# A fused decoder layer (32 batches, one core): the first and last steps in new orders

## What is computed

```python
x = _layernorm(x + _L0_attn_ref(x, L0_attn_W))                       # 1
x = _layernorm(x + _L0_xattn_ref(x, ctx_1024, ctx_1024, mask, Wq, ...)) # 2
x = _layernorm(x + _L0_ffn_ref(x, L0_ffn_Wr, L0_ffn_Wi, L0_ffn_Wo))  # 3

def _L0_attn_ref(x, W):                 # self attention without projections
    probs = softmax(x @ x.T / 16)
    vacuum_mask = probs < 0.01
    casimir = broadcast(sum of the masked probs) @ W.T
    sparse_probs = where(vacuum_mask, 0, probs), divided by its sum + 1e-9
    return sparse_probs @ x + casimir * 0.01

# 2: q, k, v projections with bias, 16 heads of 16, mask, softmax, output projection
# 3: 8 experts, the best 2 of a softmax over xf @ Wr; x @ Wi[e] @ Wo[e], weighed by their gates
```

## Time and profile before

| | |
|---|---|
| median of 3 runs (lowest, highest) | 748.14 us (746.77, 750.72) |
| the profiled execution: device time, span from first to last instruction | 752.42 us, 750.6 us |
| PE busy | 724.8 us (97%) |
| DVE, ACT, POOL busy | 662.9 (88%), 588.6 (78%), 213.5 (28%) us |
| mean granted TensorE clock | 0.992 of full |
| moved by DMA | 110.84 MB, mean 148 GB/s |

### The profile page before, as it was taken

One profiled execution on the slowest core, in us unless ns is written; L12 is line 12 of the kernel. 1 busy time (PEld: TensorE's weight loads), 2 busy tenths in 40 slices (PEclk: granted clock), 3 DMA queues, 4 the chain that ended last, 5 costly groups with the idle time before them and its releaser, 6 DMA issues.

```text
span 750.6 us, 21145 instructions
## 1 busy us (share of the span) xinstructions
PE 724.8 (97%) x7250; PEld 653.6 (87%) x7250; DVE 662.9 (88%) x2608; ACT 588.6 (78%) x1435; POOL 213.5 (28%) x384
## 2 busy tenths in 40 slices
PE   5889999999999999999999999999999999999996
PEld 4678899999999989999999989999999989889875
DVE  5587889999999889999999989999999989998976
ACT  2378989888888898888888898888988898778730
POOL 7131322133333231333331233333313333341001
PEclk9999999999999999999999999999999999999989
DMA  8865664556655565555555566556545665554100
GB/s 242 245 171 150 190 167 123 152 146 161 163 134 160 142 167 150 146 154 147 156 149 139 152 170 164 142 153 154 142 139 147 163 167 164 133 164 126 29 16 28
DMA packets 75660, 110.84 MB, mean 148 GB/s; under 512 B 14225, under 2 KB 59169, under 8 KB 75553
## 3 DMA queue, kind: packets, MB, share of 16 engines
q1 hardware_dynamic: 75552, 109.49, 54.2%
HBM read 50.23 MB, written 18.35 MB: 91 GB/s over the span
## 4 chain that ended last, share of the span: by engine, by line
PE 88%; SPq 4%; DMA 3%; DVE 3%; ACT 1%; issue 1%; POOL 0%; POOLq 0%; DVEq 0%; ACTq 0%
PE psum L1623 20%; PE psum L1397 12%; PE psum L1431 11%; PE psum L1415 10%; PE psum L1502 4%; PE psum L1490 4%; PE psum L1477 4%; PE psum L1572 3%; PE psum L1535 3%; PE psum L1513 3%; PE psum L1524 3%; SPq L393 2%; PE psum L1553 2%; PE psum L1452 2%; PE psum L1441 2%; DMA k_stack<-k_hi 1%
## 5 line engine op out<-in xcount | busy, mean ns | idle before, releaser
L934 DVE CUSTOM_DVE_ANT_0 scores_left<-psum,mask_add 112x375 f32<-112x375 f32 x512 | 270.5, 542 | 24.6 <-PE psum L1397 17.9
L613 ACT ACTIVATE probsT<-psum 125x448 f32<-125x448 f32 x384 | 201.7, 537 | 17.8 <-PE psum L1415 14.1
L598 ACT ACTIVATE psum<-mask_u 125x448 f32<-125x448 uint8 x372 | 198.2, 541 | 3.7
L1397 PE MATMUL psum<-k_stack,q_stack 96*112 96x376 f32 x512 | 183.1, 365 | 2.6 <-DMA k_stack<-k_hi 1.2
L1415 PE MATMUL psum<-q_stack,k_stack 97*125 97x224 f32 x768 | 148.2, 280 | 2.3 <-ACT psum L598 1.1
L1415 PEld LDWEIGHTS psum<-q_stack,k_stack 97*125 97x125 f32 x768 | 134.7, 188 | 13.1 <-ACT psum L598 2.5
L1166 DVE SCALAR_TENSOR_TENSOR late<-psum,gate,late 128x256 f32<-128x256 f32 x224 | 107.8, 481 | 21.0 <-PE psum L1623 12.3
L562 POOL TENSOR_TENSOR ctx_lo<-ctx_sb,ctx_hi 128x188 fp32r<-128x188 f32 x128 | 71.5, 590 | 126.4 <-ACT ctx_hi L721 126.3
L1397 PEld LDWEIGHTS psum<-k_stack,q_stack 96*112 96x112 f32 x512 | 89.1, 177 | 13.0 <-issue 6.3
L1623 PE MATMUL psum<-we_hi,x_hi 128*128 128x512 f32 x224 | 92.0, 411 | 0.5 <-DVE gate_nmax L1111 0.5
L1623 PE MATMUL psum<-we_hi,x_lo 128*128 128x512 f32 x224 | 89.0, 397 | 0.0
(11 more groups left out here) (169 smaller groups left out, 1622.3 us busy)
## 6 DMA issues: line engine op xcount, KB each, us to landing
k_stack<-k_hi SPq DMA_DIRECT2D x256, 94.0 KB, 2.6
q_stack<-q_scratch SPq DMA_DIRECT2D x96, 224.0 KB, 3.8
ctx_sb<-in_context_T SPq DMA_DIRECT2D x32, 376.0 KB, 3.7
k_stack<-k_lo SPq DMA_DIRECT2D x128, 94.0 KB, 2.5
q_scratch<-q_hi SPq DMA_DIRECT2D x32, 224.0 KB, 2.1
q_scratch<-q_lo SPq DMA_DIRECT2D x32, 224.0 KB, 2.0
xT<-in_x_T SPq DMA_DIRECT2D x32, 112.0 KB, 2.4
x_sb<-in_x SPq DMA_DIRECT2D x32, 112.0 KB, 2.9
```

The source lines that it names most:

```text
L598: nc.scalar.activation(psum[0:KP, ST_BANKS[i % 2], 0:4 * TOK].rearrange("p (h q) -> p h q", h=4), mask_u8[b % MASKS][:, KEYS + t * TOK:KEY ...
L613: nc.scalar.activation(probsT[:, place, i % KT, :], psum[0:KP, ST_BANKS[i % 2], 0:4 * TOK], ACT.Exp, scale=-1.0).then_inc(probs_ready, 1)
L934: nc.vector.tensor_tensor_reduce(scores_left[:, n % 2, :], psum[0:TOK, S_BANKS[n % 2], 0:KEYS], mask_add[b % 2][:, :], 1.0, 3.0e38, ALU.ad ...
L1397: nc.tensor.matmul(psum[0:TOK, S_BANKS[n % 2], 0:KEYS_EVEN], q_stack[s][0:96, pair, odd, c, :], k_stack[s][0:96, pair, c, :], start=True, ...
```

## The change

No arithmetic of the result changes. In the head:

- POOL fills only two of the `k_stack` rows; ACT fills the third as its first instruction, by a copy of a constant (`last_fill_of_ones`, 1 x 3008 elements). The two kinds of fill get semaphores of their own.
- SP loads `W` of stage 1 as the fourth transfer, where the context of batch 0 was; the context goes to the place behind the key weights. `load_context(b)` waits from batch 2 on for `ctx_lo(b - 2)`.
- POOL's `var1(0)`, `rstd1(0)` stand ahead of `low_context(0)`; DVE's `split_keys()` goes from ahead of `column_sums()` to behind `mom1(0)`.
- PE's `open_blocks()` goes behind `att(0)`.

In the tail: `m3(25)` goes behind two score blocks; `weigh_values(31, 0)` and `x2T_(30)` go later, `lg(26)` goes behind `weigh_values(31, 1)`; `m0(26)` is cut into halves around `aT(31)`; `m1(26)` goes behind `Wo(31)`, `m3(26)` behind `x2T_(31)`; both `run_idle(5)` go; `m1(27)` comes ahead of `m0(27)`. ACT and DVE follow: `x2_hi(30)` and `gate_exp(26)` move behind exponents and `o_sb(31)`, `attn_rest(31)` ahead of tile 26's experts, `y2(31)` two experts earlier, `x2_lo(31)` ahead of experts 6 and 7.

```diff
@@ sync
             def load_context(b):
+                if b >= 2:
+                    sp.wait_ge(done["ctx_lo"], b - 1)
...
             sp.dma_start(const_sb[:, :], consts).then_inc(consts_in, 16)
-            load_context(0)
-            rows(wk_sb, wk, wk_in)
             sp.dma_start(attn_wT[:, :, :], attn_w_T.rearrange("(c p) n -> p c n", p=128))\
               .then_inc(attn_w_in, 16)
+            rows(wk_sb, wk, wk_in)
+            load_context(0)
             rows(wv_sb, wv, wv_in)
@@ gpsimd
-            fill_ones(0); fill_ones(1); fill_ones(2); low_context(0); var1(0); rstd1(0); low_context(1); ...
+            fill_ones(0); fill_ones(1); var1(0); rstd1(0); low_context(0); low_context(1); ...
@@ scalar
+            def last_fill_of_ones():
+
+                act.wait_ge(setup_pool, 1)
+                nc.scalar.activation(
+                    k_stack[STACKS - 1][96:97, :, :, :].rearrange("o n c k -> o (n c k)"),
+                    minus_half[96:97, :].broadcast_to([1, PAIRS * DC * KEYS_EVEN]), ACT.Copy, scale=-2.0)\
+                      .then_inc(act_filled, 1)
...
-            exponent(31, 9); x2_hi(30); exponent(31, 10); exponent(31, 11); gate_exp(26); o_sb(31); attnT(31)
+            exponent(31, 9); exponent(31, 10); exponent(31, 11); x2_hi(30); o_sb(31); gate_exp(26); attnT(31)
@@ vector
-            sparse_r(0); split_keys(); column_sums(); x_cas(0); y1(0); stats1(0); mom1(0); normalize_x1(0)
+            sparse_r(0); column_sums(); x_cas(0); y1(0); stats1(0); mom1(0); split_keys(); normalize_x1(0)
...
-            expert(26, 0); attn_rest(31); expert(26, 1); expert(26, 2); expert(26, 3); y2(31); stats2(31)
-            mom2(31); expert(26, 4); expert(26, 5); normalize_x2(31); expert(26, 6); expert(26, 7); x2_lo(31)
+            attn_rest(31); expert(26, 0); expert(26, 1); y2(31); stats2(31); mom2(31); expert(26, 2)
+            expert(26, 3); normalize_x2(31); expert(26, 4); expert(26, 5); x2_lo(31); expert(26, 6); expert(26, 7)
@@ tensor
-            def run_idle(count):
-
-                pe.wait_ge(max_ready, HEADS * BATCH)
-                for _ in range(count):
-                    nc.tensor.matmul(psum[:, S_BANKS[0], 0:DIM * 2], we_hi[:, 0, 0:128], we_hi[:, 0, 0:DIM * 2],
-                                     start=True, stop=True, skip_group_check=True)
...
-            def mix_experts(t, name):
+            def mix_experts(t, name, first=0, last=3 * DC):
...
-                for n, (c, x_part, w_part) in enumerate(parts):
+                for n, (c, x_part, w_part) in list(enumerate(parts))[first:last]:
...
-            Sc(0); open_blocks(); sum_attn_w(); PT(0); att(0); x1T_(0); Sc(1); qT(0); expert_product(0)
+            Sc(0); sum_attn_w(); PT(0); att(0); open_blocks(); x1T_(0); Sc(1); qT(0); expert_product(0)
...
-            mx1(31); m1(25); Wo(30); score_block(31, 4); score_block(31, 5); m2(25); m3(25)
-            score_block(31, 6); score_block(31, 7); weigh_values(31, 0); score_block(31, 8)
-            score_block(31, 9); x2T_(30); score_block(31, 10); score_block(31, 11); lg(26)
-            weigh_values(31, 1); oT(31); m0(26); aT(31); m1(26); Wo(31); m2(26); m3(26); x2T_(31); run_idle(5); lg(27)
-            m0(27); m1(27); m2(27); m3(27)
+            mx1(31); m1(25); Wo(30); score_block(31, 4); score_block(31, 5); m2(25)
+            score_block(31, 6); score_block(31, 7); m3(25); score_block(31, 8); score_block(31, 9)
+            weigh_values(31, 0); score_block(31, 10); score_block(31, 11); x2T_(30)
+            weigh_values(31, 1); lg(26); oT(31)
+            mix_experts(26, "m0", 0, 3); aT(31); mix_experts(26, "m0", 3, 6); Wo(31); m1(26); m2(26)
+            x2T_(31); m3(26); lg(27); m1(27); m0(27); m2(27); m3(27)
```

25 lines of the change are left out of this document (14 added, 11 removed).

## The result

| | before | after |
|---|---|---|
| median of the runs on the same chips (lowest, highest, runs) | 749.57 us (746.77, 752.00, 13) | 755.42 us (752.39, 885.22, 13) |
| the profiled execution, span | 752.42, 750.6 us | 757.05, 755.3 us |
| PE busy | 724.8 us (97%) | 724.8 us (96%) |

The ratio is 1.0076, 95% interval 1.0058 to 1.0093: the change costs 5.7 us (4.3 to 7.0). One run of the changed kernel took 885.22 us at a mean granted clock of 0.751; it is left out of the ratio, and without it the median is 754.9 us. Forecast was no difference, 747.2 us; the time lies above my range.

The account below looks back on a forecast made before the run. PE, 97% busy, bounds the kernel, so only head and tail count: 752.42 - 0.9 + 0.0 = 751.5 us, or 747.2 on the median of 748.14. Own range 746.0 to 748.5, with rivals 744.8 to 750.0.

Parts of the forecast that it names:

- the head: Up to the first scores: SP freed 1.85 us sooner, but DMA takes little more; gain 0.9 us, bounds 0 to 1.85.
- the tail: Last steps up to cross(27): gain without idle products against loss at the gate; about 0, bounds -1.0 to +1.9 us.
- The reference of the tail: aT(31) ran at 729.70 in the profiled kernel before; with the change at 729.3 to 729.8, so nearly the same start.
- The exponents: Score blocks of batch 31: weigh_values(31, 0) between them makes the steps 0.2 us late.
- The gate: lg(26) behind weigh_values(31, 1): rden(31), o_norm(31) wait for tile 26's gate; o_norm over at 729.2 to 729.8, not 728.09.
- Rival C: Tail: PE idles two us ahead of aT(31), clock half through m1(26), m2(26); +1.9 us, total 749.1; chance 0.2.
- x2 to cross(27): Idle products come back as DVE work, experts 6, 7 and stats3(26): cross(27) 0.2 us later than 738.82.
- The half clock behind the pause: Behind PE's two idle us ahead of aT(31): one stretch of half clock, costing Wo(31) and half m0(26) 1.3 us more.
- Rival D: The change does nothing in the head, where drain alone sets the time; tail 0; 748.1 us; chance 0.1.
- The marker: Tail, start of weigh_values(31, 1) to cross(27), 15.1 us before: under 13.5 or over 17.5 would show the prediction wrong.
- C to its end: Half clock reaching m1(27) and m0(27) too, 12 products adding 2.3 us: 751.4 us; slower by over 0.5% had 0.06.

Follow-up runs that it names:

- h_all: Kernel before with only the change's head edits, tail as before: 749.54 us, ratio 1.0006 to the kernel before.
- t_lg: Kernel before with the change's tail edits only, but lg(26), x2T_(30), x2_hi(30) and gate_exp(26) in their old places: 750.21 us, ratio 1.0011 to before.
- o_lg: Kernel before with only lg(26), x2T_(30) moved behind weigh_values(31, 1), and x2_hi(30), gate_exp(26) with them: 751.30 us, ratio 1.0025 to before.
- t_m3: Kernel before without idle products, m3(26) behind x2T_(31), experts 6 and 7 of tile 26 behind x2_lo(31): 750.25 us, ratio 1.0007 to before.
- t_fill: Kernel before with the change's tail edits only, plus 7 unread products in the pause ahead of aT(31): 754.09 us, ratio 1.0058 to before.

## Why the prediction was wrong

**The size of the miss.** From 747.2 to 754.9 us are 7.7. The sum had the head 0.9 too good and the tail 4.6: 2.8 for the stretch it was held against, 1.8 on the path itself. The base was 1.4 too low, as 748.14 was the median of 3 runs and 13 give 749.57. The 0.7 that is left is within the noise.

**The reference of the tail (2.8 us).** "In the kernel before `aT(31)` ran at 729.70, so the start is nearly the same" is the step that failed most. I saw half clock in that very stretch and took it as a property of the kernel. It was that execution's: six of eight profiles with this order pass it at full clock and have `aT` 2.1 us sooner. Against that disturbed tail the change lost 1.83 us at `cross(27)` (28.23 - 26.40), which is inside my bounds of -1.0 to +1.9, though not by my reasons (below); against the undisturbed one 4.62 (28.23 - 23.61). I had even noted that this execution was 4.3 us above the median, and scaled the sum instead of asking where these 4.3 us lay. Against the median of 13 runs it was 2.85 late, as much as its tail.

**The path against the undisturbed tail.** The 4.62 us split at the columns of the table, after less `h_all`:

| step | predicted | measured |
|---|---|---|
| `weigh_values(31, 0)` between blocks, at exp | +0.2 | +1.09 |
| tile 26's gate ahead of `rden(31)`, to `o_norm` | late by 1.1 to 1.7 in all | +1.80 more, 2.89 in all |
| half `m0(26)` ahead of `aT(31)` | less in the way | -0.41 |
| `aT` to `y2` | -0.5 to -1.4, half clock +1.3 | +0.46 |
| `y2` to `x2` (experts 2, 3 ahead) | in the sum | +0.36 |
| `x2` to `cross(27)` | +0.2 | +1.32 |

*The exponents.* I took 0.2 us for the weighing's place between the blocks, and asked only who waits for PE's time. I did not ask what the moved step frees: the place in `probsT` for exponents 9 to 11. With it, mask, product and the last exponents are 1.1 us late.

*The gate.* The mechanism was right, and so were the absolute times: `o_norm` over at 729.2 to 729.8 predicted; measured 712.42 + 17.16 + 0.42 = 730.0. In part this is luck: the last weighing began 1.1 us later than before, not 0.2, but took 1.34 us in place of the 1.89 that I had partly counted on. PE paused 1.68 us, two predicted. Rival C was this mechanism, with chance 0.2 and a price of 1.9 us. `t_lg` gives 4.4 us back, `o_lg` costs 1.9.

*x2 to cross(27).* The swap of idle products for experts was right at 0.2 (`t_m3`: 3.77 for 3.56). Missing was a bank. `x2T_(31)` writes the bank that `m2(26)` wrote; it is free when expert 5 has read it, and the change puts experts 4 and 5 behind `normalize_x2(31)`. It starts 1.20 us behind the end of `normalize_x2` in after, 0.05 in `h_all`. I listed the experts in DVE's row and never asked which bank each releases. That is the other 1.1 us. `t_lg` has the same wait, and `t_m3`, which leaves experts 4 and 5 ahead of `normalize_x2(31)`, hasn't; a run of the change with only these two moved back was not made.

**The half clock behind the pause** came as forecast, from 17.5 to 20.9, which is up to 733.3 on the clock of the profile before. Rival C was to decide from half clock past 733, but meant all of `m1(26)` and `m2(26)` at half clock; only the first product of `m1(26)` was. It is worth 1.5 us by the profiles and 0.5 by the medians (`t_fill`), against C's 1.9.

**The head: 0.9 us predicted, none found** (the first scores 0.28 us sooner in `h_all`). `self_p(0)`, `x_cas(0)` and `load_x(2)` came as predicted. "Then SP is not held at all" failed: `expert_weights(0)` waits for all seven weights, and the last of them lands with the queue's bytes at 12.6 to 12.8. In the kernel before, this wait was hidden behind the one for `x_cas(0)`. Nor had I priced what PE's earlier work leaves behind: in three of four profiles a pause of 2 to 4 us ahead of the first scores, and half clock behind it. Rival D (drain alone) was right for the head. I had let four pieces of `ctx_lo(0)` hold `x1(0)` for 2.3 us as the worst case; it took 0.66 us in place of 0.41. By the Trainium skill ("SBUF — State Buffer", two separate sides) the lock is held for one instruction, so one piece and not the row of four is what it allows, and the trace agrees with that.

**The marker.** From `weigh_values(31, 1)` to `cross(27)` I gave 13.5 to 17.5 us as the bounds of being right. After has 743.45 - 727.59 = 15.9, so it did not warn. It was built on the disturbed 15.1; `h_all` has 12.3. And 1.1 us of the loss lies ahead of its start.

**The chances.** Slower by over 0.5% had 0.06. C to its end (751.4) was the only way there that I saw, and even that lay outside my range of 744.8 to 750.0. Two terms that I had at 0.2 or nothing, a place in a ring and a bank, cost 1.1 us each.

## What to carry to other kernels

Before a sum is made against a stretch of a profile, ask whether that stretch ran at the clock it runs at mostly: compare it with the median of the runs, and if the profiled run is late, look for the lateness there first. A step that is moved later is priced by all that its end releases, the bank it reads and the place in a ring that it frees as much as its result; each has a waiter of its own. And work taken off a critical path by delaying a second chain's input (here tile 26's logits) comes back when an in-order engine serves both chains: here, moving the steps on that engine moved the wait to the next step.

## What I had not expected of the hardware

- With the same list of instructions up to `aT(31)`, two of eight profiles had a stretch of half clock there, of 3.4 and 6.9 us, and six had none; why, no row shows. Over all tails such stretches were 3.4 to 10.2 us long. The runs of one kernel lie some 5 us apart, and go with the mean granted clock: 751.1 us by median at 0.990 and less, 748.1 at 0.994 and more.
- Transfers issued 1.5 us sooner landed at the same time (24.77 and 24.81 us): they took 6.58 us, not 5.16, for the same 224 KB.
- A copy of one partition x 3008 elements took 2.70 us on ACT and a fill of the same size 2.63 on POOL, and ACT takes 0.82 us for 128 x 752 elements. A row four times as long took 3.3 times as long, with a thirty-second of the elements: in these rows it is the length of one partition's row that counts.
